# Three short-range attentions: scores and values as 64 matmuls over 32 tokens in place of 16 over 128

## The reference

```python
x = x + xattn0(layernorm(x), ctx, ctx)   # 16 heads of 64; causal: a query of 32 tokens sees the first 32 of 257 context rows
x = x + attn0(layernorm(x))              # 16 heads of 64; causal; output times sigmoid(x @ w_gate.T)
x = x + moe0(layernorm(x))               # 64 experts, top 8
x = x + xattn1(layernorm(x), ctx, ctx)   # 16 heads of 64, all 257 context rows
x = x + attn1(layernorm(x))              # 16 heads of 32; rotary positions; scores + slope * -|i - j|
x = x + moe1(layernorm(x))               # 8 experts, top 2

def attention(q, k, v):                  # per sequence and head
    scores = einsum('bhqd,bhkd->bhqk', q, k) / sqrt(d)
    scores = scores + bias_or_mask
    return einsum('bhqk,bhkd->bhqd', softmax(scores), v)
```

## Time and profile before

| | us |
|---|---|
| median of 3 runs (lowest, highest) | 2567.41 (2563.87, 2572.26) |
| the profiled execution, its own time | 2562.45 |
| its span | 2560.5 |
| TensorE matmul busy | 2345.3 (92%) |
| VectorE busy | 1221.5 (48%) |
| ScalarE busy | 313.9 (12%) |
| `xattn0`, from the start to the next stage's first turn | 309.3 |
| `attn0` | 329.1 |
| `attn1` | 192.6 |

### The profile page before, as it was taken

The page is one execution under the profiler, slowest core; times in us unless marked ns, Lnnn a source line. Parts: engine busy times, 40 slices in busy tenths (PEclk is TensorE's granted clock), DMA queues, the critical chain, the costliest instruction groups (busy, mean ns, idle before and its releaser), DMA issues. The chain is left out here.

```text
span 2560.5 us, 39743 instructions
## 1 busy us (share of the span) xinstructions
PE 2345.3 (92%) x14730; PEld 1708.0 (67%) x14730; DVE 1221.5 (48%) x3175; ACT 313.9 (12%) x745; POOL 220.7 (9%) x266
## 2 busy tenths in 40 slices
PE   6999899999259999999979999999999997879999
PEld 5887788987148888888856766766766754444443
DVE  4777444424654444444434444444543547753333
ACT  0000011110001111111112221221221211100000
POOL 0000000000013343343310000000000000000000
PEclk8999999999569999999989999999999999989999
DMA  6114410000519999999951111011011150000000
GB/s 246 61 64 165 134 52 0 0 0 9 222 36 340 323 333 329 330 331 329 330 165 58 34 49 50 32 49 57 25 49 57 34 206 11 0 1 8 8 8 8
DMA packets 64664, 290.96 MB, mean 114 GB/s; under 512 B 9079, under 2 KB 9591, under 8 KB 55264
## 3 DMA queue, kind: packets, MB, share of 16 engines
q1 hardware_dynamic: 46976, 247.50, 26.8%
q0 software_dynamic: 16480, 40.62, 6.2%
q10 hardware_dynamic: 1152, 2.10, 0.2%
HBM read 268.45 MB, written 23.13 MB: 114 GB/s over the span
## 5 line engine op out<-in xcount | busy, mean ns | idle before, releaser
L486 PEld LDWEIGHTS psum<-work,arena 128*128 128x128 f32 x3072 | 355.7, 193 | 31.7 <-issue 30.8
L486 PE MATMUL psum<-work,arena 128*128 128x128 f32 x3072 | 356.3, 276 | 1.4 <-ACT work L1270 1.4
L295 PEld LDWEIGHTS psum<-work,arena 128*128 128x128 f32 x2560 | 294.7, 195 | 9.6 <-issue 4.8
L295 PE MATMUL psum<-work,arena 128*128 128x128 f32 x2560 | 296.1, 278 | 3.3 <-ACT work L1213 1.7
L1213 ACT COPY work<-psum 128x512 f32<-128x512 f32 (+2 forms) x216 | 112.0, 544 | 1059.4 <-PE psum L258 843.0
L665 PE MATMUL psum<-arena,work 128*128 128x512 f32 x512 | 236.2, 625 | 0.0
L560 PE MATMUL psum<-work,arena 128*128 128x257 f32 x1024 | 229.1, 381 | 0.8 <-DVE arena L1076 0.8
L581 PE MATMUL psum<-work 128*128 128x512 f32 x512 | 225.7, 594 | 2.9 <-ACT work L1213 2.2
L301 PE MATMUL psum<-arena,work 128*128 128x512 f32 x448 | 201.7, 600 | 15.4 <-DVE x L794 14.0
L560 PEld LDWEIGHTS psum<-work,arena 128*128 128x128 f32 x1024 | 191.8, 190 | 29.2 <-issue 1.2
L665 PEld LDWEIGHTS psum<-arena,work 128*128 128x128 f32 x512 | 102.0, 201 | 127.9 <-issue 127.9
(11 more groups left out here) (172 smaller groups left out, 2285.6 us busy)
## 6 DMA issues: line engine op xcount, KB each, us to landing
arena<-in_experts SPq DMA_DIRECT2D x64, 2304.0 KB, 9.9
work<-in_ctxT SPq DMA_DIRECT2D x32, 514.0 KB, 4.2
work<-in_ctx SPq DMA_DIRECT2D x32, 512.0 KB, 3.6
work<-in_ctx_tail SPq DMA_DIRECT2D x32, 450.0 KB, 3.4
arena<-in_experts SPq DMA_DIRECT2D x8, 1024.0 KB, 16.5
arena<-in_qkv SPq DMA_DIRECT2D x1, 6144.0 KB, 18.2
arena<-in_o SPq DMA_DIRECT2D x2, 2048.0 KB, 19.5
arena<-in_q SPq DMA_DIRECT2D x1, 2048.0 KB, 8.7
```

Of the source, the lines that this page charges most:

```text
L295: done = nc.tensor.matmul(to[:, n * P:(n + 1) * P], w[:, j, at:at + P], src[:, j * P:(j + 1) * P], start=(j == 0), stop=(j == KD - 1))
L486: done = nc.tensor.matmul(to[:, n * P:(n + 1) * P], w[:, at:at + P], xgT[e % 2][:, j * P:(j + 1) * P], start=(j == 0), stop=(j == KD - 1))
```

## The change

`scores` and `values` make one matmul per head and sequence: 64 of 32 by 32 tokens in place of 16. The scores of one sequence go to its own 32 partitions; row group `r` of the array (heads with the same place in a chunk) writes to its own bank, each bank 32 x chunks columns wide. So the blocks of use lie side by side over all 128 partitions, and VectorE takes them with one instruction and turns them with one. `pT` shrinks from 2048 to 512 columns and needs no zeros. In `values` sequence `b` writes to bank `SCORE + b`, and `take_out` puts the four banks in order. The scale 1/sqrt(dh) moves from the extraction into the queries: into the bias step in `xattn0`, into ScalarE's copy in `attn0`; `attn1` had it elsewhere already. In `attn0` ScalarE adds the 1 to the gate's tanh in an instruction of its own, with a semaphore `gate_ready` that `take_out` waits for. Each block has a no-op ahead of it that holds the wait. The counts of semaphores follow.

```diff
@@ -141,7 +141,7 @@
         (ctxh, qT, kT, v, gT, oT, s, pT, tail0, tail1) = carve(
-            work, 2 * D, D, HD, HD, HD, HD, HD, H * S, H * P, KD * TAIL, KD * TAIL)
+            work, 2 * D, D, HD, HD, HD, HD, HD, H * S, H * S, KD * TAIL, KD * TAIL)
         tail = [tail0, tail1]
@@ -319,14 +320,16 @@
                 wait(pe, s_o_ready, c.o.value())
-                for h in range(H):
-                    ch, off = divmod(h * st.dh, P)
-                    n = st.places.index(h)
-                    done = nc.tensor.matmul(bank[SCORE + n // 4][:, n % 4 * P:(n % 4 + 1) * P],
-                                            qT[off:off + st.dh, ch * P:(ch + 1) * P],
-                                            kT[off:off + st.dh, ch * P:(ch + 1) * P], start=True, stop=True)
-                    if n % 4 == 3:
-                        done.then_inc(s_s, 1)
+                pe.nop(nofuse=True)
+                for ch in range(st.chunks):
+                    for b in range(SEQS):
+                        own = slice(ch * P + b * S, ch * P + (b + 1) * S)
+                        for r in range(st.rows):
+                            rows = slice(r * st.dh, (r + 1) * st.dh)
+                            done = nc.tensor.matmul(bank[SCORE + r][b * S:(b + 1) * S, ch * S:(ch + 1) * S],
+                                                    qT[rows, own], kT[rows, own], start=True, stop=True)
+                            if ch == st.chunks - 1 and b == SEQS - 1:
+                                done.then_inc(s_s, 1)
@@ -338,15 +341,19 @@
             def values():
-                c.pt.add(4)
+                c.pt.add()
                 wait(pe, s_pt, c.pt.value())
-                for h in range(H):
-                    n = st.places.index(h)
-                    ch, r = divmod(h, st.rows)
-                    done = nc.tensor.matmul(psum[r * st.dh:(r + 1) * st.dh, SCORE * BANK + ch * P:SCORE * BANK + (ch + 1) * P],
-                                            v[:, h * st.dh:(h + 1) * st.dh], pT[:, n * P:(n + 1) * P], start=True, stop=True)
-                    if h >= H - st.rows:
-                        done.then_inc(s_o, 1)
+                pe.nop(nofuse=True)
+                for ch in range(st.chunks):
+                    for b in range(SEQS):
+                        own = slice(b * S, (b + 1) * S)
+                        for r in range(st.rows):
+                            h, n = ch * st.rows + r, r * st.chunks + ch
+                            done = nc.tensor.matmul(bank[SCORE + b][r * st.dh:(r + 1) * st.dh, ch * S:(ch + 1) * S],
+                                                    v[own, h * st.dh:(h + 1) * st.dh], pT[own, n * S:(n + 1) * S],
+                                                    start=True, stop=True)
+                            if ch == st.chunks - 1 and b == SEQS - 1:
+                                done.then_inc(s_o, 1)
                 c.o.add()
@@ -417,7 +424,7 @@
             pe.wait_ge(s_w[st.loads["out"]], 16)
-            counts = [(c.xn, 1), (c.proj, st.per_proj), (c.tp, st.per_tp), (c.pt, 4), (c.o, 1)]
+            counts = [(c.xn, 1), (c.proj, st.per_proj), (c.tp, st.per_tp), (c.pt, 1), (c.o, 1)]
             if st.cross:
@@ -754,10 +761,10 @@
                     def biased(src):
-                        to, bias = {"q": (qT, bq0), "k": (kT, bk0)}[which]
-                        return nc.vector.tensor_tensor(
-                            to[:, part].rearrange("p (n c) -> p n c", n=4), src.rearrange("p (n c) -> p n c", n=4),
-                            bias[:, 4 * half_:4 * half_ + 4].unsqueeze(2).broadcast_to([P, 4, P]), ALU.add)
+                        to, bias, scale = {"q": (qT, bq0, st.dh ** -0.5), "k": (kT, bk0, 1.0)}[which]
+                        return nc.vector.scalar_tensor_tensor(
+                            to[:, part].rearrange("p (n c) -> p n c", n=4), src.rearrange("p (n c) -> p n c", n=4), scale,
+                            bias[:, 4 * half_:4 * half_ + 4].unsqueeze(2).broadcast_to([P, 4, P]), ALU.mult, ALU.add)
@@ -802,16 +809,15 @@
                 sv = s.rearrange("p (h n) -> p h n", h=H)
-                c.s.add(4)
+                c.s.add(st.rows)
                 wait(dve, s_s, c.s.value())
-                for b in range(SEQS):
-                    own = slice(b * S, (b + 1) * S)
-                    src = psum[own, SCORE * BANK:(SCORE + 4) * BANK].rearrange("p (h n) -> p h n", h=H)[:, :, own]
-                    if st.rope:
-                        nc.vector.tensor_tensor(sv[own], src, alibi[own].rearrange("p (h n) -> p h n", h=H), ALU.add)
-                    else:
-                        mask = (blockmask if st.cross else causal)[own].unsqueeze(1).broadcast_to([S, H, S])
-                        nc.vector.scalar_tensor_tensor(sv[own], src, st.dh ** -0.5, mask, ALU.mult, ALU.add)
+                own = s.rearrange("p (r n) -> p r n", r=st.rows)
+                src = psum[:, SCORE * BANK:(SCORE + st.rows) * BANK].rearrange("p (r n) -> p r n", r=st.rows)[:, :, 0:st.chunks * S]
+                mask = alibi.rearrange("p (h n) -> p h n", h=H) if st.rope else (
+                    blockmask if st.cross else causal).unsqueeze(1).broadcast_to([P, H, S])
+                nc.vector.tensor_tensor(own.rearrange("p r (c n) -> p r c n", n=S), src.rearrange("p r (c n) -> p r c n", n=S),
+                                        mask.rearrange("p (r c) n -> p r c n", r=st.rows), ALU.add)
+
                 dve.drain()
@@ -832,21 +838,21 @@
                 dve.drain()
-                for b in range(SEQS):
-                    own = slice(b * S, (b + 1) * S)
-                    nc.vector.transpose(pT[own].rearrange("p (h n) -> p h n", h=H)[:, :, own], sv[own]).then_inc(s_pt, 1)
+                nc.vector.transpose(pT, s).then_inc(s_pt, 1)
                 after()
...
             def take_out():
-                c.tp.add(st.per_tp)
                 c.o.add(st.rows)
                 wait(dve, s_o, c.o.value())
-                src = psum[:, SCORE * BANK:SCORE * BANK + st.width]
+                src = psum[:, SCORE * BANK:(SCORE + SEQS) * BANK].rearrange("p (b n) -> p b n", b=SEQS)[:, :, 0:st.chunks * S]
+                src, to, gv = (src.rearrange("p b (k n) -> p b k n", n=S),
+                               *(a[:, 0:st.width].rearrange("p (k b n) -> p b k n", b=SEQS, n=S) for a in (oT, gT)))
                 if st.gated:
-                    wait(dve, s_tp_free, c.tp.value())
-                    nc.vector.scalar_tensor_tensor(oT, gT, 1.0, src, ALU.add, ALU.mult).then_inc(s_o_ready, 1)
+                    c.gate.add()
+                    wait(dve, s_gate, c.gate.value())
+                    nc.vector.tensor_tensor(to, gv, src, ALU.mult).then_inc(s_o_ready, 1)
                 else:
-                    nc.vector.tensor_copy(oT[:, 0:st.width], src).then_inc(s_o_ready, 1)
+                    nc.vector.tensor_copy(to, src).then_inc(s_o_ready, 1)
@@ -886,13 +892,13 @@
-            if not st.gated:
-                nc.vector.memset(pT, 0.0)
             if st.rope:
...
                 dve.wait_ge(s_w["bias_qk0"], 16 * 2)
+                nc.vector.tensor_scalar(bq0, bq0, DH ** -0.5, None, ALU.mult)
+                dve.drain()
             first()
@@ -1202,13 +1210,15 @@
-        def act_take(act, c, to, tanh=False):
+        def act_take(act, c, to, tanh=False, scale=None):
...
                 done = nc.scalar.activation(to, src, ACT.Tanh, scale=0.5)
+            elif scale is not None:
+                done = nc.scalar.activation(to, src, ACT.Copy, scale=scale)
             else:
@@ -1221,15 +1231,17 @@
                 if st.gated:
-                    for to in (qT, kT):
+                    for to, scale in ((qT, st.dh ** -0.5), (kT, None)):
                         for half_ in range(st.halves):
-                            act_take(act, c, to[:, half_ * BANK:(half_ + 1) * BANK])
+                            act_take(act, c, to[:, half_ * BANK:(half_ + 1) * BANK], scale=scale)
...
                         act_take(act, c, gT[:, half_ * BANK:(half_ + 1) * BANK], tanh=True)
+                    act.drain()
+                    nc.scalar.activation(gT, gT, ACT.Identity, bias=1.0).then_inc(s_gate, 1)
                 if st.rope:
```

9 lines of the change are left out of this document (6 added, 3 removed).

## The result

| | before | with the change |
|---|---|---|
| median (lowest, highest), us | 2568.96 (2563.87, 2572.26), 4 runs | 2522.32 (2520.1, 2530.89), 4 runs |
| ratio, 95% interval | | 0.9829 [0.9808, 0.9851] |
| the profiled execution, its span | 2560.5 | 2521.2 |
| TensorE matmul busy | 2345.3 | 2324.2 |
| VectorE busy | 1221.5 | 1116.2 |

The account below looks back on a forecast made before the run. TensorE bounds the wide attentions; TensorE and VectorE alternate in rope. 11.8 + 2.1 + 12.7 + 5.4 + 24 + 5.6 + 4.5 = 66 us, less 3 for the sequencer: net 63, median 2504; own range 2488 to 2522, whole to 2582.

Parts of the forecast that it names:

- VectorE, 4.3 us a tile: Softmax in each attention tile: one extraction and one turn at about 0.70 us each replace four each, saving 4.3 us.
- The lower end of the range for new patterns: VectorE's extraction and turn: if the patterns with more dimensions double their cost, the saving is 2.9 us a tile.
- TensorE, 1.1 us a block: Scores and values blocks: 128 pairs at 7 ns plus about 0.2 us, 1.1 us in place of 1.99 and 1.90.
- A floor per matmul: Rival for TensorE's blocks: each pair costs 30.6 ns, a wide block 3.9 us, net +58 us, 2625; chance 0.19.
- Half the pieces: Rival for TensorE's blocks: only two matmuls run together, a block takes 2.0 us, net 32 us saved, 2535; chance 0.18.
- The wide attentions: Cross-attention and gated attention up to their last scores: shorter scores and values save 11.8 and 12.7 us.
- the gated one: Gated attention's end: the 3.07 us wait for the turn goes and the values save 2.3, together 5.4 us.
- it gains the extraction's 2.1 us: End of `xattn0`: the path runs through the copy behind the extraction, then the rest rows' trip to memory, saving 2.1 us.
- Rope, one period: Rope attention's 22.85 us period: turn's 1.7, extraction's 2.1 and scores' 0.1 to 0.2 save 4.0 us; six periods, 24 us.
- TensorE's own way has about 0.7 us of slack, so it is late next: Rope period: values, value projection and turns on TensorE would be the next limit, with about 0.7 us to spare.
- the first tile: Rope attention's first tile: the key rotation starts 3.5 us earlier and the next extraction gives 2.1, together 5.6 us.
- The rope end: End of rope attention: turn 2.2, values 0.8, projection 1.5 if the clock stays up; together 4.5 us saved.

Follow-up runs that it names:

- the order experiment: Changed kernel with the same 64 matmuls reordered, chunk innermost, so 8 (rope: 4) in a row go to one piece of the array: 2697.14 us, ratio 1.0518.
- the second profile: The changed kernel measured once more without any edit, with a profile that shows no pause: 2528.38 us, ratio 0.9856.
- the edit of the kernel before: Kernel before the change, with the rope attention's second addition to x moved ahead of the four turns: 2556.61 us, ratio 0.9966.
- the fill: Changed kernel plus three unused 256-column matmuls in TensorE's wait ahead of the rope scores: 2517.94 us, ratio 0.9804.
- the two repeats: Changed kernel once more, 2528.38 us (0.9856), and with 96 no-ops added that left no record, taken as a third copy, 2527.52 us (0.9859).
- the copy moved: Changed kernel with the rope attention's output copy ahead of the layer norm on VectorE: 2511.75 us, ratio 0.9795.

## Why the prediction was right, and by how much it was off

**VectorE, 4.3 us a tile: right.** 0.69 and 0.71 us. The lower end of the range for new patterns did not come up.

**TensorE, 1.1 us a block: right in kind, 0.1 to 0.3 us too low.** 1.23 and 1.42 us. The argument, that neighbours on different pieces start within 10 ns, is borne out by the order experiment: with the neighbours on one piece (and in one bank) the pair costs 21 to 46 ns. The rival "A floor per matmul" had 30.6 ns and blocks of 3.9 us; those blocks exist, but only in that order. The rival "Half the pieces", 2.0 us a block, is refuted by the 1.23.
The Trainium skill, "TensorE: Matmul & The Clock Gate", section on the clock gate (the matmul gap), has at least about 25 ns between starts; this case's trace does not agree across pieces, with 128 pairs in 1.23 us. Its section on packing small matmuls has matmuls start and end strictly in program order. With the two passes of each matmul directly one behind the other that would be "Half the pieces"; the 1.23 us shows that the two together do not hold, and no run here shows the order by itself.

**The wide attentions: right but for the blocks' price.** A tile was to lose 1.69 us and lost 1.39 and 1.25; over the two stages 19 us in place of 24.5 (13.5 in the second profile). The ends: the gated one gave 4.1 of 5.4 where the low clock went on into the projection, and 5.8 in the second profile, where it did not. For `xattn0` the step "it gains the extraction's 2.1 us" failed: last scores to last values is 2.9 us shorter (13.61 to 10.74), but the stretch behind it is 4.8 longer, 3.1 of them absent in the execution without a pause (22.57 against 19.45). There the path is the one the prediction named, and the rest of the loss lies in it: from the copy L865 (278.38) to the correction (297.85) the rest rows take 19.5 us, before 17.2. The end then gives 1.2 of the 2.1 us.

**Rope, one period: the step that failed.** The prediction let the extraction and the turn save 2.1 and 1.7 us a period and added them, to 18.9. The turn's term was right: the addition behind it held the key projection, as the edit of the kernel before shows (22.85 to 21.2). The extraction's term took the query projection as starting 0.9 us behind the addition, wherever that moved. But the output projection L365 ends just 0.9 us before it; once this gap was gone, TensorE's own ring of scores, output, query and key projections, then rotation, norm and copy, was the longest at 19.8 us. "TensorE's own way has about 0.7 us of slack, so it is late next" named the values, the value projection and the turns and left that ring out. In the traces the way from the scores to the query projection shrank from 6.14 to 5.15 us, 1.0 in place of 2.1, and the scores in it cost 0.1 us more where 0.1 to 0.2 less were forecast; the way from there to the key rotation shrank from 9.19 to 7.07, 2.1 in place of 1.7. Together 3.1 us in place of 4.0, so 0.9 us a period are missing.
For the same reason the first tile gained 3.6 us (21.06 to 17.45), the key rotation's share, and nothing from the extraction: 2.0 us short.
The second part is the clock: 1.5 us in three of the periods, shown by the fill (140.57 to 135.88). Together 6 x 0.9, 2.0 and 3 x 1.5 make 11.9 us; 11.5 are missing.

**The rope end: wrong in sign in this profile.** Forecast -4.5, measured +1.9; without the pauses -6.6 (21.19 to 14.60). So the terms of the turn and of the clock were right in kind, and the pauses hid them. The prediction took 0.1 us a block for the sequencer and nothing for running out of instructions. The four times longer blocks are four times as many instructions, and the profile shows 49 blocks on the instruction queue, 36 before.
The Trainium skill, "Runtime: NRT & Kernel Launch", section Instruction fetch mechanics, calls the cost of crossing such a block mostly hidden. Here it was hidden in the loops and in one profile of three of this program, and was 2 to 9 us in the others.

**The net.** 63 us forecast, 35 to 47 measured. The whole range (2488 to 2582) held; of the forecast's own part of it, up to 2522, the first median stands at the edge and the two repeats (2527.5 and 2528.4) outside. The largest term, the rope attention's 29.6 us, came out at 18, and for a reason that the prediction did not name, so what is confirmed is the direction, VectorE's price and the kind of TensorE's, not the sum.

## What to carry to other kernels

Small matmuls paid here where heads are 64 wide and neighbours in the program go to different pieces of the array; with heads of 32 they gave TensorE nothing, and with neighbours on one piece they lost. Put the piece in the innermost loops. When two engines hand work to each other, write down the ring of each engine with all its members before adding up what parts save, since two savings that hide behind the same work are not additive and an order of one instruction can be worth as much as the change. Straight code of many small instructions at a stage's end can run ahead of its fetching, above all while the DMA engines are full, and one profile doesn't tell whether it does.

## What was not expected of the hardware

- 128 pairs of 32 columns over 8 or 16 pieces go in 1.21 to 1.42 us; in another order in 2.6 (16 pieces), 3.47 and 8.2 us (8 pieces), and during the last the granted clock falls to 0.50 although the engine is never idle.
- Instructions that come late cost 2.05 us by themselves and 8.87 behind transfers that hold the DMA engines 95%. The same program had all three pauses in two profiles and none in a third. Each break looked at ends 2 to 3 us behind the landing of an instruction block; at the end of `xattn0` the block landed some 4 us or more ahead of the values in the five profiles looked at that have no break there. What decides it stays open.
- 1.41 us of idle time ahead of the small scores brought the lower clock in three or four of seven periods; 0.77 us, with the copy moved, brought it in none. With the matmuls in the other order and the same 0.77 us it still fell in one (an output projection of 5.95 us in place of 3.62).
- Stages that no edit touches took 13 us longer in one execution of the changed kernel than in another (1474.4 and 1461.0 us from the end of `attn0` to the rope attention's first scores), more than the 8.5 us that its rope end gained.
